# Orders in a hand-scheduled attention and routing loop: reciprocal first, product behind the fourth maximum, count ahead of the projection half

## The reference

```python
x = x + xattn(layernorm(x), ctx, ctx, mask, Wq, bq, Wk, bk, Wv, bv, Wo, bo)
#   q, k, v = split_heads(...); probs = softmax(q k^T / sqrt(16), masked); attn = probs v; attn @ Wo.T + bo
x = x + ffn(layernorm(x), Wr, W1, W2)
#   t = tokens; probs = softmax(t @ Wr); idx = argmax; pmax = max
#   pos = (tokens before this one that chose the same expert); kept = pos < 640
#   eout = relu(ein @ W1) @ W2 per expert; out = where(kept, pmax * eout[slot], t)
```

## Time and profile before

| | |
|---|---|
| median of 3 runs | 554.75 us (554.36 to 555.15) |
| the profiled execution's own time | 556.13 us |
| its span, first to last instruction | 554.4 us |
| mean granted TensorE clock | 0.923 of full |
| busy: PE, PEld | 466.1 us (84%), 313.5 us (57%) |
| busy: DVE, ACT, POOL | 207.3, 152.3, 190.4 us |
| busy in row maxima (L807) | 46.3 us |

### The profile page before, as it was taken

How to read it: one execution, slowest core, us unless ns; L and a number is a source line. 1 busy time by engine, 2 the same in 40 slices (tenths; PEclk the granted TensorE clock), 3 DMA queues, 4 the chain that set the end, 5 groups by cost and what they waited for, 6 DMA issues and landing times.

```text
span 554.4 us, 7679 instructions
## 1 busy us (share of the span) xinstructions
PE 466.1 (84%) x2823; PEld 313.5 (57%) x2823; DVE 207.3 (37%) x590; ACT 152.3 (27%) x224; POOL 190.4 (34%) x306
## 2 busy tenths in 40 slices
PE   5797869699999999968243399999999999999991
PEld 2342234253434343423132288999989989899891
DVE  5853336355656565544242123112131121313110
ACT  0145515535554646344101111101001010111000
POOL 4671603408585766060626202111101111221221
PEclk9999979889999999968575589999999999999997
DMA  6992633614232333333402406015060060624000
GB/s 202 321 273 93 192 95 91 201 45 143 83 134 96 123 109 106 119 106 120 148 0 80 145 1 214 28 44 187 19 204 29 20 218 20 214 95 145 6 30 0
DMA packets 51658, 62.35 MB, mean 112 GB/s; under 512 B 4658, under 2 KB 41561, under 8 KB 51616
## 3 DMA queue, kind: packets, MB, share of 16 engines
q1 hardware_dynamic: 46560, 53.53, 30.4%
q0 software_dynamic: 3456, 7.26, 3.7%
q10 hardware_dynamic: 1600, 1.01, 0.7%
HBM read 32.17 MB, written 27.41 MB: 107 GB/s over the span
## 4 chain that ended last, share of the span: by engine, by line
PE 67%; DMA 9%; DVE 8%; SPq 7%; issue 4%; POOL 3%; ACT 1%; ACTq 0%; POOLq 0%; DVEq 0%
PE tps L1317 11%; PE wk L1327 10%; PE tps L1337 10%; PE wk L1345 9%; PE wk L1185 6%; SPq L399 6%; PE wk L1097 5%; PE nat L1117 5%; DMA attn_mem<-rsum 4%; PE tps L1139 3%; PE wk L1169 3%; DMA strips<-shared 2%; DVE rowmax L807 2%; DVE attn_mem L836 2%; PE nat L1305 1%
## 5 line engine op out<-in xcount | busy, mean ns | idle before, releaser
L588 POOL DMA_INDIRECT out_x<-attn_mem,dest x40 | 39.0, 975 | 198.6 <-DVE attn_mem L1014 195.8
L623 ACT ACTIVATE shared<-tps,mask_key 77x1024 f32<-77x1024 f32 x64 | 67.5, 1104 | 28.9 <-PE tps L1143 28.9
L807 DVE TENSOR_REDUCE rowmax<-nat 128x8 f32<-128x616 f32 x58 | 46.3, 798 | 51.6 <-PE nat L1117 50.6
L1117 PE MATMUL nat<-kblk,qT 64*128 64x308 f32 x232 | 47.0, 481 | 16.5 <-DVE rowmax L807 16.5
L1317 PE MATMUL tps<-shared,w_sb 128*128 128x256 f32 x256 | 59.7, 393 | 0.6 <-ACT shared L679 0.6
L1327 PE MATMUL wk<-w_sb,shared 128*128 128x256 f32 x256 | 57.7, 379 | 0.0
L1337 PEld LDWEIGHTS tps<-shared,w_sb 128*128 128x128 f32 x480 | 56.0, 192 | 0.8
L1337 PE MATMUL tps<-shared,w_sb 128*128 128x128 f32 x480 | 56.0, 275 | 0.0
L1317 PEld LDWEIGHTS tps<-shared,w_sb 128*128 128x128 f32 x256 | 50.7, 198 | 8.4 <-issue 1.0
L1345 PE MATMUL wk<-w_sb,shared 128*128 128x256 f32 x240 | 54.3, 379 | 0.0
L1327 PEld LDWEIGHTS wk<-w_sb,shared 128*128 128x128 f32 x256 | 48.1, 190 | 6.3
(11 more groups left out here) (136 smaller groups left out, 522.8 us busy)
## 6 DMA issues: line engine op xcount, KB each, us to landing
w_sb<-in_w SPq DMA_DIRECT2D x16, 1024.0 KB, 8.4
strips<-shared SPq DMA_DIRECT2D x32, 256.0 KB, 3.7
slot_rows<-zeros SPq DMA_DIRECT2D x1, 5200.0 KB, 25.7
x_sb<-slot_rows SPq DMA_DIRECT2D x8, 650.0 KB
x_sb<-in_x SPq DMA_DIRECT2D x8, 512.0 KB, 8.9
attn_mem<-strips SPq DMA_DIRECT2D x32, 128.0 KB
attn_mem<-rsum SPq DMA_DIRECT2D x64, 64.0 KB
out_x<-base SPq DMA_DIRECT2D x8, 512.0 KB, 3.1
```

What stands on the lines that cost most here:

```text
L588: pool.indirect_dma_start(out_rows, bass.IndirectOffsetOnAxis(ap=dest[n % 2][:, c:c + 1], axis=0), y_sb[n % 2][:, c, :], None, bounds_chec ...
L623: act.activation(probsT[0:SK, r % 2, 2 * i:2 * i + 2, :], tps[0:SK, 2 * i:2 * i + 2, :], ACT.Exp, bias=mask_key[:, g // GPB:g // GPB + 1]) ...
L807: dve.tensor_reduce(rowmax[:, j, :, m, :], nat_heads(g, k), AX.X, ALU.max).then_inc(rowmax_ready, 1)
L1117: last = pe.matmul(dst, qT[g % 2][of, m, j * P:(j + 1) * P], kblk[of, b, m, :, :].rearrange("p (i r) k -> p i (r k)", i=2), start=True, st ...
```

## The change

It changes three orders in the passes and one wait:

- VectorE: `invert_sums(r)` stands ahead of `second_norm(o)` and of the first row maximum, instead of behind the first row maximum. ScalarE's `copy_attn` waits for the landing of the earlier group's sums instead of for their reciprocal.
- VectorE: `normalise_attn(r)` stands behind row maximum 3 instead of ahead of it. TensorE: `natural_scores(n, 3)` stands ahead of `weigh_values(c, 1)` instead of behind it.
- TensorE: `count_before(o)` stands ahead of `project(r, 1)` instead of behind natural scores 7. VectorE: `masked_positions(o)` stands ahead of `add_residual(r, 1)` instead of behind row maximum 7.

No operation is added or taken away.

```diff
--- before.py
+++ after.py
@@ copy_attn (ScalarE)
                 wait(act, strip_stored[r], 16 * g)
-                wait(act, rsum_ready, g)
+                wait(act, sums_loaded, 16 * ROUNDS * g)
@@ step (VectorE)
+                if has(r):
+                    invert_sums(r)
                 if has(o):
                     second_norm(o)
                 if has(n):
                     row_maxima(n, 0)
-                if has(r):
-                    invert_sums(r)
-                if has(n):
                     row_maxima(n, 1)
                 if a == 1:
                     first_norm(1)
                 if has(n):
                     row_maxima(n, 2)
+                    row_maxima(n, 3)
                 if has(r):
                     normalise_attn(r)
-                if has(n):
-                    row_maxima(n, 3)
                 if has(o):
                     choose(o)
...
                     row_maxima(n, 5)
                     row_maxima(n, 6)
+                if has(o):
+                    masked_positions(o)
                 if has(r):
                     add_residual(r, 1)
                 if has(n):
                     row_maxima(n, 7)
-                if has(o):
-                    masked_positions(o)
-                if has(n):
                     split_maxima(n)
@@ step (TensorE)
                 if has(o):
                     router_logits(o)
+                if has(n):
+                    natural_scores(n, 3)
                 if has(c):
                     weigh_values(c, 1, a, o)
-                if has(n):
-                    natural_scores(n, 3)
                 if has(c):
                     scores(c, 2)
...
                 if has(n):
                     natural_scores(n, 6)
+                if has(o):
+                    count_before(o, c)
                 if has(r):
                     project(r, 1, c, o)
                 if has(n):
                     natural_scores(n, 7)
                 if n == 0:
                     values(2)
-                if has(o):
-                    count_before(o, c)
```

## The result

| | before | after |
|---|---|---|
| median of 4 runs each | 554.95 us (554.36 to 555.57) | 548.44 us (547.59 to 549.16) |
| ratio of the times, 95% interval | | 0.9882 (0.9864 to 0.990) |
| the profiled execution, its span | 556.13, 554.4 us | 547.59, 545.8 us |
| mean granted TensorE clock | 0.923 | 0.921 |
| busy: PE, DVE, ACT, POOL | 466.1, 207.3, 152.3, 190.4 us | 462.0, 206.0, 151.5, 190.3 us |

The change is 6.5 us faster (1.2%). The two profiled executions stand 8.6 us apart in span: that of before (556.13) is longer than each of the four runs beside it, and that of after is the shortest of its four. When the changed kernel ran again beside the experiments (e9), the ratio was 0.9823 (0.978 to 0.9866), 10.5 us. The forecast of 8.25 lies between the two.

The account below looks back on a forecast made before the run. TensorE fills most slices, so only its waits, about 1.7 us per full pass, can give time. Full passes 2.85, the pass after 1.7, weight passes 3.6, tail 0.1: 8.25 us off 554.75, 546.5 us; range 545 to 548, whole 542.5 to 550.

Parts of the forecast that it names:

- likeliest case: Whole kernel: the forecast itself, 8.25 us off the median to 546.5 us, own range 545 to 548, chance 0.50.
- Product behind the fourth maximum: Full passes: with natural scores 3 moved earlier, the projection starts 1.15 us earlier and does not wait for the product.
- Count ahead of the half: Second projection half: the count no longer covers the residual wait, so the pass is 0.2 us longer, bounds 0 and 0.28.
- Reciprocal first: VectorE, full passes: natural scores 1 come 0.2 us late, broadcasts land at 163.0 instead of 165.88, no gain in full passes.
- I take the sums as landed by then: VectorE, full pass: sums have landed by 154.86, so the reciprocal at VectorE's head waits for no transfer.
- rival (b): Late sums hold the reciprocal at VectorE's head; total gain about 5 us, 549.8 us; chance 0.12.
- (c): Rival: SyncE's strips or another queue bound the shorter pass, each full pass keeps half, 549 to 550 us; chance 0.10.
- I count nothing: ScalarE's copy of round 0 comes some 0.7 us earlier, but its next work waits for TensorE, so no gain.
- The passes with weights: Broadcasts land as before; fourth maximum and natural scores 4 fill the wait; 1.6 and 2.2 less 0.2, 3.6 us in all.
- 1.2 us remain: First weight pass, case where half rate still ends at 80.2: 1.2 of the 2.05 us gain is left.
- Rival (a): TensorE's clock stays up in one or both weight passes: 2 to 4 us more, 542.5 to 544.5 us; chance 0.21.
- The tail: Groups 6 and 7 to normalise: nothing comes earlier, only the count ahead of the last addition gives 0.1 us.

Follow-up runs that it names:

- e9: The changed kernel run again with no edit, beside the last three experiments: 545.87 us, ratio 0.9823 to the kernel before.
- e2: Kernel before with only the product moved behind row maximum 3 and natural scores 3 ahead of the second attention product: 548.65 us, ratio 0.987.
- e3: Kernel before with only the count and the masked positions moved as in the changed kernel: 559.2 us, ratio 1.0042 to the kernel before.
- e8: Changed kernel with the reciprocal and ScalarE's wait put back, so product and count alone are moved: 545.86 us, ratio 0.9805 to the kernel before.
- e5: Changed kernel with SyncE's packs issued one round later, behind the next round's gather and store: 545.37 us, ratio 0.9805 to the kernel before.
- e12: e11 with the reciprocal and ScalarE's wait back as in the kernel before: 536.96 us, ratio 0.965 to the kernel before.
- e11: Changed kernel with e5's later packs, e10's late weights, and count and masked positions in their old places: 530.43 us, ratio 0.954 to the kernel before.
- e7: Changed kernel with the experts' weights issued behind instead of ahead of the broadcasts in the two weight passes: 543.98 us, ratio 0.9757 to the kernel before.
- e10: Changed kernel with the first two experts' weights issued behind the loop's last broadcasts: 536.7 us, ratio 0.9628 to the kernel before.

## Why the prediction was right, point by point

**In short.** The time came within the whole range, but two signs that the prediction had set for its being wrong came true. VectorE's reciprocal waits for a DMA in full passes, and a half-rate stretch appears where none was, in group 7's second projection half. The full passes are 27.26 and 27.93 us instead of the 27.35 forecast for all. The terms that held are the product's new place, the count and the order in the weight passes; what failed is named below.

**The total.** 546.5 forecast, 548.44 measured: 0.4 us above the likeliest case's own range (545 to 548) and inside the whole one (542.5 to 550). I took 8.25 us off; the two comparisons give 6.5 and 10.5. The profiled pair gives 8.6, but its two executions lie at opposite ends of their runs, so that its sum agrees so well is partly luck. It agrees, too, because errors of both signs cancel: the lead at group 2 is 0.75 us more than forecast, the full passes from there to group 4 add 1.4 where I had 1.9, and the pass to group 5 adds 2.1 instead of 1.7.

**Product behind the fourth maximum: right.** Natural scores 4 wait for no maximum, natural scores 3 keep the "about 0.4 us" (0.42 measured), the product stands behind the maximum, the projection never waits for it. I had this part and the 0.2 us price of the early reciprocal in one number, 1.15. e2, which has no early reciprocal, measures 28.30 - 26.95 = 1.35, which is the same sum without the 0.2. Its product waits for the later broadcasts and is still in time, as the prediction had said of this case.

**Count ahead of the half: right.** Predicted 0.2 us a pass, measured 0.13 (e3) and 27.09 - 26.95 = 0.14 (e8 against e2). It is a loss and buys nothing here, and the best version has the count in its old place.

**Reciprocal first: two terms wrong, with opposite signs.** The step "I take the sums as landed by then" failed. It was rival (b), to which I gave 0.12, mixed with (c). I had argued from the strips' 2.1 us and put SyncE's slack before the last gather at about 1 us; the trace had 1.80. The 2.1 us was the landing of the last round, which this slack keeps clear of a pack; the strips right behind a pack took 3.69 us in the same trace, and the gather of the earlier trace rows, with its 4.05 us, was issued 0.04 us behind one (263.98 to 264.02). The shorter pass uses up the slack, the last gather then stands right behind a pack and lands after 3.87 us. Of the passes to groups 3 and 4, the one with a wait of 0.36 us wins 1.04 and the one with 1.16 us wins 0.37, where I had 0.95 for both. Against the 26.79 of e5 the second loses 1.14, about 1 us for each us of wait. e5, which only moves SyncE's packs one round back, makes both 26.8: that is the cause shown.

The other failed term is "I count nothing" for ScalarE's wait. Before, the copy of the attention waits for the reciprocal and holds the second half of the transposes (timeline of the kernel before, then after):

```profile
159.15 1.39 PE L1204 MATMUL wk<-ident,t_sb 128*128 128x128 f32 x8
159.25 0.58 ACT L631 COPY shared<-wk 128x512 f32<-128x512 f32 x1 [1.73 <-DVE rsum L830]
```

```profile
153.14 0.59 ACT L631 COPY shared<-wk 128x512 f32<-128x512 f32 x1 [0.98 <-PE wk L1166]
...
154.26 1.09 PE L1201 MATMUL wk<-ident,t_sb 128*128 128x128 f32 x8
```

The prediction called everything but the two waits "back to back"; a group of matmuls that is held in its middle shows no idle time, only a longer one. With the sums in time the part gains 0.3 us a pass instead of costing 0.2: 27.09 in e8 and 26.79 in e5. That 28.30 - 1.35 + 0.14 - 0.30 gives 26.79 proves nothing, since the terms are differences of these same passes; that e12 and e11 differ by the same 0.3, and the transposes by 1.39 - 1.09, does. So "the early reciprocal adds nothing" holds for the changed kernel as it is, where late sums eat the 0.3 us (e8 against e9), and falls once they are in time (e12 against e11). Whether ScalarE's wait alone, with the reciprocal in its old place, would give the 0.3 us was not tried.

**The passes with weights: the order right, one size off.** Predicted starts of the projection 74.94, and 3.65 us of lead at group 1; measured 74.58 and 3.64. The broadcasts in the first land where they did (product 73.18, before at 73.5), behind the same weights, though they are begun 2.65 us earlier. In the Trainium skill, DMA: Bandwidth & Descriptors (Queues, rings and completion order) says that each DMA engine takes its descriptors in ring order; this trace agrees, and e7 agrees from the other side, where the broadcasts go ahead of the weights and no product waits for them. The clock was between my cases. In the first pass half rate lasted the 6.8 us as before, "1.2 us remain", and 84.15 - 83.03 = 1.1 did, where I had taken 1.6. In the second it lasted 3.4 us instead of 6.8, and the lead at the third round of scores (115.83 to 111.83, 4.0 us, of which 1.1 were brought from the pass before) is 2.9 us from this pass instead of 2.2. The two errors nearly cancel, 4.0 against 3.8 us. Rival (a), a clock that stays up, did not come about; e10 shows what it is worth together with the wait, 7.0 us in the two passes.

**The tail: a size off.** "0.1 us" was the term; in the profiled pair the lead goes from 9.0 at group 5 to 10.0, to 8.7, to 7.5 at the experts' start and 8.6 at the end. Timeline of VectorE and TensorE with group 7:

```profile
259.06 0.94 DVE L830 RECIPROCAL rsum<-sums 64x128 f32<-64x128 f32 x1 [4.48 <-DMA sums<-shared]
...
269.21 3.78 PE L1182 MATMUL wk<-wo_sb,attn_mem 128*128 128x256 f32 x8 [3.36 <-DVE attn_mem L836]
```

Group 7's reciprocal waits 4.48 us for its sums (0.46 before, when VectorE came to it later), and group 7's projection halves take 3.78 us each after, and 3.78 and 1.99 before: half rate in the second too. At the experts it is the other way round: the first expert's first 32 matmuls take 9.01 instead of 10.16 us. I had called this about 1 us either way. I hold these stretches for the likeliest source of the 4 us between the two comparisons too, but that is argued, not shown.

## What to carry to other kernels

Before an operation goes to the head of an in-order engine, ask when its input lands once the pass has become shorter: slack that is read from the old trace (here 1.8 us on SyncE) is the first thing that the gain uses up. A landing time read from the one transfer that has this slack ahead of it (2.1 us) is not the landing time without it (3.7 us). Follow a moved wait one engine further, to the buffer that the waiting engine has yet to free: early reciprocal and ScalarE's wait together were worth 0.3 us a pass with the sums in time, and the trace puts it at the buffer that ScalarE holds; the one line on ScalarE was not tried alone. And when a large transfer delays a small one, moving it just behind the small one moves the wait to the next pass (e7, 0.9757); moving it behind the last small ones is worth much more (e10, 0.9628).

## What the runs showed of the hardware

- The 8 KB gather of the sums, issued 0.04 us after a 128 KB pack on the same queue, landed after 3.87 us; 0.27, 1.4 and 2.4 us after one it landed after 3.63, 2.66 and 1.75 us (kernel after), and 5.7 us after one also after 1.75 us (e5). The strips landed after 2.2 us in the median in e5 and 3.6 in the kernel after.
- Eight broadcasts of 64 KB took 5.2 us to issue when nothing large stood ahead of them (e7) and 8.25 us right behind 2 MB of weights. Begun 2.65 us earlier, they were all issued only 0.32 us earlier.
- In the weight passes of the kernel after, TensorE stood for 3.77 us, its clock fell 0.8 us before the end of that wait and stayed at 1.2 GHz for 6.8 us. The second time it stood for 2.59 us, and the clock fell 1.3 us behind the wait, for 3.4 us. With the weights elsewhere (e10) it was busy 1.01 of the 2 us from 66 to 68 and all of the 6 us behind them, and its clock stayed at 2.4 GHz.
- Between executions of one kernel the time varied by 1% and more, and the longest had the lowest mean granted clock: 529.12 us at 0.937 and 535.64 us at 0.925 in e11. So the 0.2% that is given at the start as what can be told from none holds for the first comparison; with six executions each the intervals here were 0.3 to 0.65% to either side.
